# Adding the causal mask to the scores in PSUM on VectorE instead of by a product on TensorE

## The reference

```python
def _L0_attn_ref(x, Wq, Wk, Wv, Wo):        # 16 heads, 4 kv heads, head dim 128
    q, k, v = x @ Wq.T, x @ Wk.T, x @ Wv.T  # split into heads, q and k rotated (_rope)
    scores = jnp.einsum('bhqd,bhkd->bhqk', q, k) * scale
    causal = jnp.triu(jnp.ones((S, S), dtype=bool), k=1)
    scores = jnp.where(causal[None, None], jnp.float32(-jnp.inf), scores)
    attn = jax.nn.softmax(scores, axis=-1)
    out = jnp.einsum('bhqk,bhkd->bhqd', attn, v)
    return out @ Wo.T                       # after the heads are laid side by side
x = x + _layernorm(_L0_attn_ref(_layernorm(x), Wq, Wk, Wv, Wo))
x = x + _layernorm(_L0_ffn_ref(_layernorm(x), ...))   # router (top 6 of 64 experts), experts, shared expert
```

## Time and profile before

| | us |
|---|---|
| median of 3 runs (2109.83, 2110.24, 2123.09) | 2110.24 |
| the profiled execution | 2121.3 |
| its span | 2119.5 |
| mean granted TensorE clock over the span | 0.935 |
| TensorE matmul busy | 1886.7 |
| VectorE busy | 1357.2 |
| ScalarE busy | 1153.3 |
| GpSimd busy | 1302.9 |

### The profile page before, as it was taken

One profiled execution on the slowest core, in us unless ns is written; L12 is line 12 of the kernel. 1 busy time (PEld: TensorE's weight loads), 2 busy tenths in 40 slices (PEclk: granted clock), 3 DMA queues, 4 the chain that ended last, 5 costly groups with the idle time before them and its releaser, 6 DMA issues. The chain is left out here.

```text
span 2119.5 us, 34272 instructions
## 1 busy us (share of the span) xinstructions
PE 1886.7 (89%) x11782; PEld 1568.5 (74%) x11782; DVE 1357.2 (64%) x3198; ACT 1153.3 (54%) x2632; POOL 1302.9 (61%) x1057
## 2 busy tenths in 40 slices
PE   5999999998999999999999999999999999776720
PEld 4888888887888888877888888877888888543310
DVE  5666666676667667666666767756666777652228
ACT  3657565655566655565665656555655555322313
POOL 5758584858566666666484757576666655215843
PEclk8999999999999999999999999999999999895655
DMA  4003000001100100000200100011001000487364
GB/s 176 12 26 101 7 20 6 21 6 51 56 21 6 41 6 26 6 31 21 66 11 11 36 6 26 6 51 35 21 6 41 16 1 26 161 327 229 58 190 148
DMA packets 74233, 111.77 MB, mean 53 GB/s; under 512 B 10790, under 2 KB 54772, under 8 KB 72928
## 3 DMA queue, kind: packets, MB, share of 16 engines
q1 hardware_dynamic: 61040, 88.42, 12.5%
q0 software_dynamic: 8544, 12.73, 2.6%
q10 hardware_dynamic: 4480, 8.44, 1.2%
HBM read 81.90 MB, written 35.47 MB: 55 GB/s over the span
## 5 line engine op out<-in xcount | busy, mean ns | idle before, releaser
L563 PE MATMUL s_ps<-kT,q 128*128 128x512 f32 (+3 forms) x2304 | 598.5, 378 | 16.8 <-ACT probs L960 8.3
L826 DVE TENSOR_TENSOR pT<-t_ps,pT 128x512 fp32r<-128x512 f32 (+3 forms) x768 | 401.6, 551 | 329.1 <-ACT pT L971 328.1
L563 PEld LDWEIGHTS s_ps<-kT,q 128*128 128x128 f32 x2304 | 409.2, 195 | 61.8 <-ACT probs L960 14.2
L588 PE MATMUL av_ps<-pT,v 128*128 128x512 f32 x1728 | 437.3, 399 | 0.0
L813 DVE TENSOR_REDUCE neg_max<-s_ps 128x1 f32<-128x640 f32 (+7 forms) x512 | 384.1, 750 | 70.5 <-PE s_ps L563 64.7
L1122 POOL TENSOR_TENSOR k_roped<-raw,sinT 64x512 f32<-64x512 f32 x316 | 406.6, 1287 | 24.3
L960 ACT ACTIVATE probs<-s_ps,neg_max 128x640 f32<-128x640 f32 (+7 forms) x512 | 381.2, 745 | 68.4 <-DVE neg_max L813 66.9
L971 ACT ACTIVATE pT<-t_ps 128x512 fp32r<-128x512 f32 (+3 forms) x768 | 348.2, 489 | 128.0 <-PE t_ps L573 122.4
L1119 POOL TENSOR_TENSOR k_roped<-raw,cosT 128x512 f32<-128x512 f32 x158 | 204.0, 1291 | 278.8 <-ACT raw L932 259.9
L588 PEld LDWEIGHTS av_ps<-pT,v 128*128 128x128 f32 x1728 | 316.0, 190 | 59.8
L573 PE MATMUL t_ps<-k_ident,probs 128*128 128x128 f32 x2304 | 341.5, 275 | 14.7 <-DVE pT L826 10.4
(11 more groups left out here) (234 smaller groups left out, 1882.0 us busy)
## 6 DMA issues: line engine op xcount, KB each, us to landing
w_early<-in_expert_w SPq DMA_DIRECT2D x5, 2560.0 KB, 26.7
k_staged<-in_wpack SPq DMA_DIRECT2D x47, 256.0 KB, 2.8
k_staged<-in_wpack SPq DMA_DIRECT2D x16, 512.0 KB, 3.7
w_early<-sums SPq DMA_DIRECT2D x16, 512.0 KB, 8.5
e_w_late<-in_expert_w SPq DMA_DIRECT2D x3, 2560.0 KB, 21.4
sums<-sums ACTq DMA_DIRECT2D x1, 4144.0 KB, 15.7
k_xw<-in_x SPq DMA_DIRECT2D x4, 1024.0 KB, 5.6
k_xb<-in_x SPq DMA_DIRECT2D x4, 1024.0 KB, 5.2
```

The lines of the kernel that those rows point to most:

```text
L563: last = pe.matmul(out, q[:, macro % 2, a, h, int(big)], kT[:, g % 2, s, lo:hi], start=(n == 0), stop=(n == 2))
L588: last = pe.matmul(av_ps[:], v[:, g % 2, a, j], pT[:, s, part_slot(p) + j], start=(j == 0 and n == 0), stop=(j == blocks - 1 and n == 2))
L826: dve.tensor_tensor(lo, t_ps[n % 2][:, 0:count * P].rearrange("p (j n) -> p j n", n=P), hi.bitcast(F32), ALU.subtract).then_inc(t_lo, 1)
```

## The change

In `scores` the mask product goes, so each last chunk has three matmuls like all others. In `row_max` VectorE first adds the bf16 mask to the diagonal tile in PSUM, in place, 128 x 128; the addition goes through `link`, so the maximum waits for its completion; then the maximum is taken as before. The identity in bf16 and its load go, and the wait for the mask moves from TensorE to VectorE.

```diff
-        ident_bf = sb("ident_bf", [P, P], BF16)
         mask_bf = sb("mask_bf", [P, P], BF16)
@@ sync
-            sp.dma_start(ident_bf[:], consts["ident_bf"]).then_inc(masks_in, 16)
             sp.dma_start(mask_bf[:], consts["mask_bf"]).then_inc(masks_in, 16)
@@ scores
                     for n, (a, s) in enumerate(((0, 0), (0, 1), (1, 0))):
-                        if n == 2 and hi == width:
-                            pe.matmul(s_ps[:, r % 2, width - P:width], ident_bf[:], mask_bf[:], start=False, stop=False)
                         last = pe.matmul(out, q[:, macro % 2, a, h, int(big)], kT[:, g % 2, s, lo:hi], start=(n == 0), stop=(n == 2))
@@ tensor
-            pe.wait_ge(masks_in, 32)
@@ vector
             def row_max(r):
+                width = (row_tile(r) + 1) * P
+                diagonal = s_ps[:, r % 2, width - P:width]
+                if r == 0:
+                    dve.wait_ge(masks_in, 16)
                 dve.wait_ge(scores_ready, r + 1)
-                dve.reduce_max(neg_max[:, r % 16:r % 16 + 1], s_ps[:, r % 2, 0:(row_tile(r) + 1) * P], AX.X, negate=True).then_inc(max_ready, 1)
+                link(dve.tensor_tensor(diagonal, diagonal, mask_bf[:], ALU.add))
+                dve.reduce_max(neg_max[:, r % 16:r % 16 + 1], s_ps[:, r % 2, 0:width], AX.X, negate=True).then_inc(max_ready, 1)
```

## The result

The change makes the kernel slower. The median of four runs is 2155.95 us (2153.06 to 2159.98) against 2112.31 us (2109.83 to 2123.09) before; the ratio is 1.0195 with a 95% interval of 1.0173 to 1.0217, +43.6 us by the medians. The profiled execution took the median time, with a span of 2153.9 us. Single macros agree far better, but for those into which a stretch at half clock falls.

The account below looks back on a forecast made before the run. TensorE's stream was taken as the bound, with waits on VectorE deciding the sign. Products saved against additions on the path gave 0.19 us a plain macro, 0.68 with stages, +24 us in all: 2134 us from 2110.24, range 2093 to 2166.

Parts of the forecast that it names:

- The three places named: TensorE's waits for L960 (exponentials), L858 and L826 (`probs_low`), said to grow by 70 to 90 us in all.
- the band of the forecast: Whole kernel: stalls a little above the saving, 2120 to 2145 us, with a chance of 0.5.
- rival C: Addition at 0.4 to 0.5 us, or product mostly hidden; deciding from 0.36 or below 0.09; 2150 to 2165 us, chance 0.23.
- Part 1: Mask product leaving TensorE: 0.12 us a row, 0.08 or 0.09 at width 128, at most 55 us over 64 macros.
- Part 2: Addition on VectorE before the maximum: 0.282 + 0.035 = 0.32 us each, 162 us more load, VectorE 77% busy.
- Part 3, plain macros: Walk of waits over a group of four macros, m = 0 to 3: +0.74 us, 0.19 a macro, 2.5 additions on the path.
- Part 3, macros with stages: Macros with top-k, norms or router on VectorE have less cover; the one at 837.46 (m = 1) grows by 0.68 us.
- only 0.6 of their 0.95 us come through: In that macro, additions of rows 0, 1 and 2 ahead of L858 delay the q projection: p = +0.60.
- The sum: All 64 macros: 3 us from batch 0, 16 and 5 us from the other 48, in all +24 us.
- A: TensorE stays the bound all the way, all 55 us come: 2055 us, or 2095 by half; chance 0.12.
- B: The addition is cheap on the path, 0.20 us: 2115 us, no measurable difference; chance 0.15 shared with one other rival.
- D: Row 0's exponentials are late through ScalarE's `probs_high`, so the addition adds no stall there: 2114 us, within a shared chance of 0.15.

Follow-up runs that it names:

- experiments 6 and 7: Against the kernel before, addition on VectorE only in row 5 of each macro (1.0060), or only in rows 0, 1 and 2 (1.0151); other rows keep the product.
- experiment 1: Kernel before with the mask product removed and no addition put in, diagonal tile left unmasked: 0.9906 of before, 20 us less.
- experiments 10 and 11: Kernel before and changed kernel, both without the top-k passes in attention batches 1 to 3: 0.9951 and 1.0093 of before, medians 2108.56 and 2140.51 us.
- experiment 3: Kernel before with the product kept on TensorE and the addition also made on VectorE: 1.0260 of before, +55 us.
- experiment 8: Changed kernel with the diagonal's chunk of scores made first in big rows, the addition running beside the other chunk: 1.0137 of before, 13 us less than the change.
- experiment 4: Changed kernel with the addition made twice, each with its wait: 1.0541 of before, 72 us over the changed kernel.

## Why the prediction was right

**The bound and the sign.** TensorE's stream was the bound, and a product off it paid only where no wait stood behind. The three places named are the ones where the time went, shown by rows (the three waits are 70 us longer) and by experiments 6 and 7, which turn on one set of places each and move only those waits. The time itself came out within the range but above the band of the forecast (2120 to 2145), where the prediction had put its rival C; the mechanism was right, two terms of the sum were too kind. That the range held is luck in part: it was as wide as it was for the prices of one addition and one product, and those were not what moved the time.

**Part 1.** The 0.12 us for a product and 0.08 at 128 columns hold where the product is on the stream, but in six of 32 rows it is not, so 49 us and not 55 could go (experiment 1). Of these only 20 arrive. The walk allowed for five masks in a macro, some 40 us. What it lacked are waits that grow once the product is gone, and they are not only in the macros with stages: batch 0 gives back 0.44 us a macro and the other batches 0.38.

**Part 2.** 0.291 + 0.033 us where I had 0.282 + 0.035. The wait on itself is there (the maximum starts 0.33 us behind the start of the addition). VectorE's load grew by 144 us, to 74% of a longer attention, where 162 us and 77% were said. The Trainium skill's "VectorE: DVE Perf Modes", section "The TRN2 errata — SBUF-src ops pay a fixed extra latency per instruction", gives (N + 151) / 0.96 ns for an fp32 tensor_tensor, by which 128 columns take an estimated 291 ns: here the trace agrees to the nanosecond, though one operand is bf16 and the output lies in PSUM. The rule of the Trainium skill, "VectorE: DVE Perf Modes", section "The DRAIN you can't avoid", that the semaphore is free, weighed in the prediction, is not what these rows show: all 512 maxima start 0.033 to 0.035 us behind the end of the addition they wait for, while VectorE instructions without such a wait start about 0.083 us before the end of the one in front.

**Part 3, plain macros.** Walked: m = 0 +0.14, m = 1 +0.04, m = 2 +0.24, m = 3 +0.32 us. Measured in batch 0, from the scores of row 0 to those of the next macro, four macros each: m = 0 -0.07, +0.33, +0.33, +0.29; m = 1 +0.19, +0.49, +0.39, -0.03 (the last is the one walked); m = 2 +0.28 to +0.33; m = 3 +0.20 to +0.50. So the walked macro came out as walked and two others with m = 1 did not. In those two the shift up to the scores of row 2 is the same, about +0.2 us, but another 0.3 comes between the scores of row 2 and those of row 3, where the output's wait for L858 shows (the loader's is 0.15 us before and 0.67 after in the second of the four); with m = 0 it is 0.2 to 0.3 in the same place. One macro with m = 1 stood for all, and it was the mildest of the four. The mean of batch 0 is 0.28 us a macro instead of 0.19.

**Part 3, macros with stages.** The one walked came out at +1.03 us instead of +0.68. The step that failed is "only 0.6 of their 0.95 us come through": the timeline shows all three.

```profile
856.90 0.30 DVE L812 TENSOR_TENSOR s_ps<-s_ps,mask_bf 128x128 f32<-128x128 f32 x1
...
857.24 1.09 DVE L813 TENSOR_REDUCE neg_max<-s_ps 128x1 f32<-128x896 f32 x1
...
858.75 0.48 DVE L858 SCALAR_TENSOR_TENSOR k_xw<-misc_ps,inv_sum,y 128x256 f32<-128x256 f32 x1
...
859.29 0.39 PE L518 MATMUL misc_ps<-xT,w_q 128*128 128x256 f32 x1 [0.86 <-DVE k_xw L858]
```

From the macro's start to the q projection it is 9.84 us, against 8.88 before: +0.96. L858 ends 9.78 us behind that start, against 8.82: later by three additions of 0.33 us, nearly whole.

**The sum.** +24 us forecast, +43.6 measured: inside the range, which was there for this, but low by 20. By macros, the two traces give 36 us. Batch 0 is +4.4 (forecast 3), batches 1 to 3 are +31.5 (forecast 21), 0.66 us a macro instead of 0.44. The other 8 us can't be placed, since the trace of before lies above its kernel's median. Two things stand behind the 10 us of batches 1 to 3, and the runs don't part them. The macros with stages are the first: without the passes the loss is 12 us smaller (experiments 10 and 11), which is what the forecast had given all stages together, 24 x (0.68 - 0.19) us. The clock is the second, which the prediction named in rival C as "a few us" and left out of the sum. The same place of macro 12 of batch 1, before and after, from the scores of row 2 to those of row 3:

```profile
811.95:819.24 7.29, 6.10 (x36) 4.86 (x34) 5.49 (x9) 2.39 (x5) 0.00 (x0) 1.00 0.01 3
```
```profile
821.20:830.60 9.40, 7.53 (x34) 6.03 (x33) 6.20 (x13) 2.33 (x5) 0.00 (x0) 0.82 0.00 1
825.20:828.60 3.40, 3.40 (x12) 2.82 (x11) 2.45 (x6) 0.00 (x0) 0.00 (x0) 0.50 0.01 2
```

Of the 2.1 us by which it grows, 0.7 are the longer wait for L858 (1.19 us before, 1.87 after). The other 1.4 fit the twelve matmuls at the lower of the two clock levels, 1.2 GHz, in the 3.4 us behind that wait, of which at most half, 1.7 us, is the clock's.

```profile
814.88 0.98 PE L600 MATMUL misc_ps<-w_o,avT 128*128 128x256 f32 x6 [1.19 <-DVE y L858]
```
```profile
824.71 0.51 PE L596 MATMUL misc_ps<-w_o,avT 128*128 128x256 f32 x2 [1.87 <-DVE y L858]
```

The stretches at half clock that begin between the first and the last scores are 44 us before and 65 after, and 75 with two additions. A stretch costs at most half its length, so the clock is up to 10 us of the loss. That the longer waits cause the stretches is argued from their place; no run held the waits and changed the clock. Longer waits do not bring them every time: in the trace of experiment 3, which is 55 us slower than before, they are 41 us.

**The rivals.** A falls by the sign, B by the size and by the addition's row (0.324 us and not 0.20). D falls by experiment 8: TensorE's wait for row 0's exponentials shrinks as soon as the addition leaves that path. It is not on that path everywhere, though: between the scores of row 0 and those of row 2 the change adds 0.21 us in the macro of the earlier trace rows, but with m = 0 it takes off 0.10 to 0.12 us in macros 4, 8 and 12 of batch 0, so there D holds. C had the number, 2150 to 2165, but not for its reasons: the addition is at 0.291 us and the product at 0.12 (0.095 over all rows), both on the forecast's side of the limits that C set, the second of them barely. Only its remark on the clock, a stretch more in each batch for a few us, came true: there are 3 to 10 us more at half clock in each of batches 1 to 3.

## What to carry to other kernels

A cheap product on the engine that is the bound can be worth less than its share of the stream, and the same work on an engine with a third of its time idle can cost more, where that engine stands between two steps of the bound: count the waits, not the load. Walk one period of the schedule from wait to wait and ask for each instruction what stands queued behind it; here one addition in eight made about a third of the loss and three others were free. Move work row by row to where the walk shows a gap. Walk more than one period, and also the stretches in which the other engine has more to do than usual: the one plain macro walked here was the mildest of its kind. A saving has to be walked as well, since work taken away lays waits bare.

## What the runs showed of the hardware that was not expected

- A bf16 product of 128 columns set between fp32r products costs TensorE's stream 0.12 us in most rows, but a second one right behind it with the same weights only 0.055 to 0.06, though its weights are loaded again.
- An addition of an SBUF and a PSUM operand written back to PSUM takes 0.291 us, against 0.282 for the row that writes to SBUF. In experiment 4 the second of the two additions, which waits for the first, takes 0.300.
- Three to ten more microseconds at half clock in each of batches 1 to 3 came with waits of TensorE that had grown by well under a microsecond each (1.19 to 1.87 us in macro 12 of batch 1); experiment 3, whose waits are longer too, had none more.
